# A transformer block with modulated LayerNorms: the attention gate row in a tile and a transfer of its own

## The chip, the cores and the metric

The kernel runs on one core of a Trainium2 chip. The metric is the device time of one execution in microseconds, as the median of several runs. All times in this document are microseconds unless marked ns.

## What is computed

For each of 32 batch entries with 256 tokens of 128 values (cut from the reference):

```python
mod = (_silu(c) @ wmod).reshape(32, 6, 1, -1)
sa, ca, ga, sb, cb, gb = (mod[:, n] for n in range(6))
ga = (2 * (ga >= 0) - 1) * jnp.maximum(jnp.abs(ga), 0.25)
gb = (2 * (gb >= 0) - 1) * jnp.maximum(jnp.abs(gb), 0.25)
h = _layernorm(x) * (1 + ca) + sa
x = x + ga * attn(h)       # rmsnorm, 16 causal heads of 64, sigmoid head gates, @ Wout
h = _layernorm(x) * (1 + cb) + sb
x = x + gb * ffn(h)        # SwiGLU MLP with bias bd, plus experts chosen by product keys
```

The six modulation rows of a batch entry are one value for each of the 128 features and hold for all its tokens. `ga` scales the output of the attention before the residual is added. The output bias `bd` of the MLP is inside the second gate, so the kernel forms `gb * bd` once (the row called GD) and adds it to the new residual.

## The kernel before

**Rows of the modulation.** All modulation rows are computed once at the start and stored to a DRAM tensor, `mods_dram`, of 32 by 7 rows of 128 values: SA, CA, GA, GD, GB and a pair of columns, in this order. In each batch the sync engine (SP) loads from it, broadcast over the 128 partitions: `modA` (SA and CA, for the first LayerNorm), `modB` (GA and GD: 1 KB per partition, 128 KB in all), `modC` (GB, 64 KB) and `col` (the second LayerNorm's columns). There is one buffer of each, so each load waits until the batch before has been read out of it.

**The pipeline.** The batches run in a software pipeline: each engine has a function `body(i)`, called for i from -1 to 32, with the work of one more body woven into the last call; the middle (from 3 on) is a hardware loop. Body i does the projections, scores and the softmax of batch i, the output projection and the second LayerNorm of batch f = i - 1, the experts and the MLP of batch g = i - 2, and the first LayerNorm of batch i + 1. Within a body the order of the work of each engine is written out by hand; semaphores tie the engines together. Matmul results go to four shared PSUM banks, `pW0` to `pW3`, in a fixed order of jobs (`order`); a job may begin when the job before it in its bank has been released. For this change it matters that the value projection `V 4` takes the bank of `GU 3` (the last of four gate and up projections), which VectorE releases with `gate_product(3)`.

**Around the gate.** On VectorE (the function under `@block.vector`) the order of body i is ... `row_max(3)`, `gated_down(0)` (line 1151), `invert(2)` (line 1124), `gate_attention()` (line 1182), `gate_product(3)` (line 1165), `add_residual()` (line 1191), `invert(3)`, `stats2()` (line 1197), `coefficients(2)`, `coefficients(3)`, `aggregate2()` (line 1205), `normalise(2)`, `normalise(3)` (line 1142), `choose(1, 1)` (line 1268, half of the expert masks of the second token block), `ln1(center1)` (line 1004), `gated_down(1)`, `ln1(scale1)` (line 1017), `row_max(4)` (line 1117). `gate_attention` waits for `modB` and for the output projection (`project_out`, line 1685 on TensorE) and multiplies the PSUM bank by row 0 of `modB`. `add_residual` adds `x_res`, the token rows loaded again for this purpose, writes `x2` and releases the bank.

After `aggregate2` GpSimd computes the reciprocal standard deviation (`rstd2`, lines 566, 567, 569 and 571), ScalarE scales the rows with it (`rows2`, line 784), and TensorE transposes them (line 1585). GpSimd's order in a body is `products(0)` (line 515), `candidates()`, `products(1)`, `weigh(0)` (line 524), `add_heads(0)` (lines 531 and 534), `add_bias()` (line 588), `fold(0)` (lines 540 and 544), `rstd1()`, `rstd2()`, `weigh(1)`, `add_heads(1)`, `rms1()` (line 558), `fold(1)`, `shift_top()`. `add_bias` adds row 1 of `modB` (GD) to `x2` of batch g and writes `x2g`, which the last step of batch g adds to the MLP's output.

**The sync queue.** SP's body i issues in this order, each step behind the waits that stand before it: (line 433) `x_in` of batch i + 2 behind `xr_ready`, (line 425) `modA` of i + 2, (line 442) `x_res` of batch i behind the release of the output projection's bank for batch i - 1, that is behind `add_residual`, (line 445) `col` of batch i behind `h2T_high`, (line 453) the store of the output of i - 2 behind the release of bank job `y`, (line 455) `modC` of i - 1, and last (line 460) `modB` of batch i behind `x2g_ready` of batch i - 1. The gate row of batch i is first read by VectorE's body i + 1 and the GD row by GpSimd's body i + 2. `add_bias` of batch i - 1, for which line 460 waits, belongs to GpSimd's body i + 1: the sync queue's body i so ends in the middle of the other engines' body i + 1, shortly ahead of the gate of batch i.

Of the kernel before, what the change touches and what calls it, by code (L numbers as in the profile page):

```python
# [12 lines left out]
ALU = mybir.AluOpType  # L13
# [3 lines left out]
B, N, D = 32, 256, 128  # L17
P = 128
TB = N // P
# [25 lines left out]
SA, CA, GA, GD, GB, COL = range(NMOD - 1)  # L45


def program(nc, x, norm_w, Wq, Wkv, Wout, Wgate, fWg, fbg, fWu, fbu, fWd, fbd, fWq, keys,
            down, up, cond, wmod, out):
    ctx = ExitStack()  # L50
    with ctx:
        def sb(name, shape, dt=F32):
            return ctx.enter_context(nc.sbuf_tensor(name, shape, dt))

        def sem(name):
            return ctx.enter_context(nc.semaphore(name))
# [42 lines left out]
        mods_dram = nc.dram_tensor("mods_dram", [B, NMOD * D], F32, kind="Internal").ap()  # L99
# [2 lines left out]
        x_in = sb("x_in", [P, TB, D])  # L102
        x_res = sb("x_res", [P, TB, D])
        modA = sb("modA", [P, 2, D])
        modB = sb("modB", [P, 2, D])
        col = sb("col", [P, 2])
        modC = sb("modC", [P, 1, D])
        st1 = sb("st1", [P, TB, 6])
# [18 lines left out]
        x2 = sb("x2", [P, TB, D])  # L127
        x2g = sb("x2g", [P, TB, D])
# [64 lines left out]
        def ev(name, n):  # L193
            s = sem(name)
            per[name] = (s, n)
            return name

        def at(name, batch, k):

            return batch * per[name][1] + k  # L200

        def S(name):
            return per[name][0]

        x_loaded, res_loaded = ev("x_loaded", 16), ev("res_loaded", 16)
        col_loaded = ev("col_loaded", 16)
        modA_loaded, modB_loaded, modC_loaded = ev("modA_loaded", 16), ev("modB_loaded", 16), ev("modC_loaded", 16)
        out_stored = ev("out_stored", 16)
        ln1_chain, inverse_ready = ev("ln1_chain", LN1_LINKS), ev("inverse_ready", NP)
        head_chain, tail_chain = ev("head_chain", HEAD_LINKS), ev("tail_chain", TAIL_LINKS)  # L210
# [178 lines left out]
        def run(eng, body, first=3, tail=1):  # L389


            for i in range(-1, first):
                body(i)
            with eng.Fori(first, B - tail) as i:
                body(i)
            for i in range(B - tail, B + 1):
                body(i)
# [3 lines left out]
        @block.sync  # L401
        def _(sp):

            sp.dma_start(x_in[:, :, :], x[0:1].rearrange("o (k p) d -> p (o k) d", p=P)).then_inc(S(x_loaded), 16)
            sp.dma_start(nw[:, :], norm_w.rearrange("(d o) -> d o", o=1), allow_slow_non_contiguous=True).then_inc(load_nw, 16)
            sp.dma_start(w_qkv[:, 0:2 * P], Wq[:, 0:2 * P]).then_inc(load_pairs, 16)
            sp.dma_start(w_qkv[:, DI:DI + 2 * P], Wkv[:, 0:2 * P]).then_inc(load_pairs, 16)
            for a in range(2):
                sp.dma_start(fwq_sb[:, :, a, :], fWq[:, a * RH * KD:(a + 1) * RH * KD].rearrange("d (h n) -> d h n", h=RH)).then_inc(load_keys, 16)
            sp.dma_start(key_sb[:, :, :], keys.rearrange("h k p n -> k h (p n)")).then_inc(load_keys, 16)  # L410
            sp.dma_start(w_qkv[:, 2 * P:DI], Wq[:, 2 * P:DI]).then_inc(load_q, 16)
            sp.dma_start(w_qkv[:, DI + 2 * P:2 * DI], Wkv[:, 2 * P:DI]).then_inc(load_k, 16)
            sp.dma_start(w_qkv[:, GV:GV + H], Wgate).then_inc(load_gv, 16)
            sp.dma_start(w_qkv[:, GV + H:], Wkv[:, DI:2 * DI]).then_inc(load_gv, 16)
            sp.dma_start(down_sb[:, :, :], down.rearrange("(c p) d -> p c d", p=P)).then_inc(load_down, 16)
            sp.dma_start(w_out[:, :, :], Wout.rearrange("(j p) n -> p j n", p=P)).then_inc(load_w, 16)
            sp.dma_start(w_g[:, :], fWg).then_inc(load_w, 16)
            sp.dma_start(w_u[:, :], fWu).then_inc(load_w, 16)
            sp.dma_start(b_g[:, :], fbg.rearrange("(c p) -> p c", p=P), allow_slow_non_contiguous=True).then_inc(load_w, 16)
            sp.dma_start(b_u[:, :], fbu.rearrange("(c p) -> p c", p=P), allow_slow_non_contiguous=True).then_inc(load_w, 16)  # L420
            sp.dma_start(w_d[:, :, :], fWd.rearrange("(c p) n -> p c n", p=P)).then_inc(load_w, 16)
            sp.dma_start(w_up[:, :, :], up.rearrange("(c p) n -> p c n", p=P)).then_inc(load_w, 16)

            def load_modA(b):
                sp.dma_start(modA[:, :, :].rearrange("p m d -> p (m d)"),
                             mods_dram[bass.ds(b, 1), SA * D:(CA + 1) * D].broadcast_to([P, 2 * D])).then_inc(S(modA_loaded), 16)

            def body(i):
                w = Work(sp, i)
                if w.live(2):  # L430

                    sp.wait_ge(S(xr_ready), at(xr_ready, i + 1, 1))
                    sp.dma_start(x_in[:, :, :], x[bass.ds(i + 2, 1)].rearrange("o (k p) d -> p (o k) d", p=P)).then_inc(S(x_loaded), 16)
                    if isinstance(i, int) and i == -1:
                        sp.wait_ge(su_dve, SU_LINKS)
                        sp.dma_start(mods_dram, mods[:, :, :].rearrange("b m d -> b (m d)")).then_inc(mods_stored, 16)
                        sp.wait_ge(mods_stored, 16)
                    load_modA(i + 2)
                if w.live(0):
                    if w.live(-1):  # L440
                        w.wait_released("op")
                    sp.dma_start(x_res[:, :, :], x[bass.ds(i, 1)].rearrange("o (k p) d -> p (o k) d", p=P)).then_inc(S(res_loaded), 16)
                    if w.live(-1):
                        sp.wait_ge(S(h2T_high), at(h2T_high, i - 1, 1))
                    sp.dma_start(col[:, :], mods_dram[bass.ds(i, 1), COL * D:(COL + 2) * D].rearrange("o (d m) -> d (o m)", m=2)).then_inc(S(col_loaded), 16)
                if w.live(-2):
                    if isinstance(i, int) and i > B:
                        for k in range(TB):
                            w.wait_released("y", k)
                            sp.dma_start(out[Z, k * P:(k + 1) * P, :], yo[:, k, :]).then_inc(S(out_stored), 16)  # L450
                        return
                    w.wait_released("y")
                    sp.dma_start(out[bass.ds(i - 2, 1)].rearrange("o (k p) d -> p (o k) d", p=P), yo[:, :, :]).then_inc(S(out_stored), 16)
                if w.live(-1):
                    sp.dma_start(modC[:, :, :].rearrange("p m d -> p (m d)"),
                                 mods_dram[bass.ds(i - 1, 1), GB * D:(GB + 1) * D].broadcast_to([P, D])).then_inc(S(modC_loaded), 16)
                if w.live(0):
                    if w.live(-1):
                        sp.wait_ge(S(x2g_ready), at(x2g_ready, i - 1, 1))
                    sp.dma_start(modB[:, :, :].rearrange("p m d -> p (m d)"),  # L460
                                 mods_dram[bass.ds(i, 1), GA * D:(GD + 1) * D].broadcast_to([P, 2 * D])).then_inc(S(modB_loaded), 16)

            run(sp, body, tail=2)
            body(B + 1)
            sp.wait_ge(S(out_stored), at(out_stored, B, 16))

        @block.gpsimd
        def _(pool):
# [24 lines left out]
            def body(i):  # L493
                w = Work(pool, i)
                f, g = i - 1, i - 2
# [86 lines left out]
                def add_bias():  # L582
                    if w.live(-2):
                        w.wait_released("op", 0, g)
                        pool.wait_ge(S(modB_loaded), at(modB_loaded, g, 16))
                        if w.live(-3):
                            w.wait_released("y", 0, g - 1)
                        nc.gpsimd.tensor_tensor(x2g[:, :, :], x2[:, :, :], modB[:, 1:2, :].broadcast_to([P, TB, D]),
                                                ALU.add).then_inc(S(x2g_ready), 1)

                if isinstance(i, int) and i == 0:
# [27 lines left out]
                weigh(0)  # L619
                add_heads(0)  # L620
                add_bias()
                fold(0)
                rstd1()
# [350 lines left out]
        def _(dve):  # L974
# [130 lines left out]
            def body(i):  # L1105
                w = Work(dve, i)
                f, g = i - 1, i - 2
# [68 lines left out]

                def gate_attention():
                    if w.has("op"):
                        dve.wait_ge(S(modB_loaded), at(modB_loaded, f, 16))
                        w.wait_full("op")  # L1180
                        o = w.bank("op")[:, 0:N].rearrange("p (k d) -> p k d", k=TB)
                        nc.vector.tensor_tensor(o, o, modB[:, 0:1, :].broadcast_to([P, TB, D]), ALU.mult).then_inc(S(head_chain), 1)

                def add_residual():
                    if w.has("op"):
# [806 lines left out]
```

## Time and profile before

| | us |
|---|---|
| median of 3 runs (lowest, highest) | 1395.2 (1394.33, 1395.93) |
| the profiled execution's own time | 1397.2 |
| its span, first to last instruction | 1395.3 |

| engine | busy, us | share |
|---|---|---|
| TensorE matmuls (PE) | 1354.7 | 97% |
| TensorE weight loads (PEld) | 1161.5 | 83% |
| VectorE (DVE) | 1251.7 | 90% |
| ScalarE (ACT) | 1261.1 | 90% |
| GpSimd (POOL) | 1067.2 | 76% |

The granted TensorE clock is 0.995 of full speed over the span, and the DMA engines moved 20 GB/s in the mean. The profile is one execution. Busy times are sums of instruction durations; matmul ends are modelled, so a busy PE is not PE at its peak. Waits are inferred from semaphore events: idle time of an engine just ahead of an instruction, put down to what ended it.

### The profile page before, as it was taken

What the parts mean: (1) busy time and instruction counts of PE and PEld (TensorE: products, weight loads), DVE (VectorE), ACT (ScalarE), POOL (GpSimd) and SP (SyncE); (2) the same over time, 40 slices, a digit from 0 to 9 for tenths busy, and PEclk for the clock granted to TensorE, in tenths of its full rate; (3) what the DMA queues carried; (4) which work ended last, traced back from release to release, by engine and by line L of the source; (5) the groups of instructions that cost most, each with busy time, mean ns of one, the idle gap of its engine ahead of it and who ended that gap; (6) DMA issues with size and microseconds to landing.
All of it is one profiled execution on the core that took longest, in us unless ns stands there. A gap on an engine that the chain in (4) does not pass through costs nothing. (4 is left out here: it accounts for less than half of the span.)

```text
span 1395.3 us, 39507 instructions
## 1 busy us (share of the span) xinstructions
PE 1354.7 (97%) x11491; PEld 1161.5 (83%) x11491; DVE 1251.7 (90%) x5314; ACT 1261.1 (90%) x4084; POOL 1067.2 (76%) x1252
## 2 busy tenths in 40 slices
PE   7799999999999999999999999999999999999998
PEld 4578888888888888888888888888888888888878
DVE  5579999999999999999999999999999999999977
ACT  5789999999999999999999999999999999999985
POOL 2148887888787888787888888888888887878770
PEclk9999999999999999999999999999999999999999
DMA  4000000000000000000000000000000000000000
GB/s 137 16 15 21 9 18 21 17 21 19 9 17 21 18 19 20 11 14 21 20 17 21 13 11 21 21 17 21 15 9 21 21 17 21 15 9 24 10 15 11
DMA packets 51041, 27.74 MB, mean 20 GB/s; under 512 B 10336, under 2 KB 50208, under 8 KB 51008
## 3 DMA queue, kind: packets, MB, share of 16 engines
q1 hardware_dynamic: 50768, 26.91, 7.3%
q10 hardware_dynamic: 240, 0.43, 0.1%
q8 instruction: 16, 0.26, 0.1%
q14 instruction: 17, 0.14, 0.0%
HBM read 23.02 MB, written 4.31 MB: 20 GB/s over the span
## 5 line engine op out<-in xcount | busy, mean ns | idle before, releaser
L692 ACT ACTIVATE pS<-pS,nmx 128x128 f32<-128x128 f32 (+1 forms) x1024 | 405.5, 500 | 17.8 <-DVE nmx L1117 16.5
L524 POOL TENSOR_TENSOR fexp<-fexp,fsum 128x512 f32<-128x512 f32 x240 | 306.3, 1307 | 75.0 <-DVE fexp L1268 75.0
L1117 DVE CUSTOM_DVE_ANT_0 pS<-pS,mask 128x128 f32<-128x128 f32 (+1 forms) x1024 | 333.6, 393 | 27.9 <-PE pS L1629 23.7
L692 ACT ACTIVATION_READ_ACCUMULATOR pS<-pS,nmx 128x1 f32 x1024 | 253.3, 256 | 0.0
L515 POOL TENSOR_TENSOR fsum<-ex 128x512 f32<-128x512 f32 x248 | 251.8, 1047 | 0.0
L1142 DVE TENSOR_TENSOR p_sb<-pS,coef 128x256 f32<-128x256 f32 (+2 forms) x512 | 206.7, 451 | 5.7
L1639 PE MATMUL pS<-ident,p_sb 128*128 128x128 f32 x1536 | 204.1, 276 | 4.3 <-DVE p_sb L1142 2.2
L684 ACT COPY pT<-pS 128x768 f32<-128x768 f32 x256 | 201.4, 850 | 6.4 <-PE pS L1639 6.2
L1639 PEld LDWEIGHTS pS<-ident,p_sb 128*128 128x128 f32 x1536 | 171.0, 141 | 27.3 <-DVE p_sb L1142 12.4
L672 ACT COPY qk<-pW 128x512 f32<-128x512 f32 x256 | 155.1, 606 | 8.4 <-PE pW L1573 3.8
L531 POOL TENSOR_TENSOR fexp<-fexp 128x512 f32<-128x512 f32 x120 | 158.7, 1343 | 4.7
L1654 PE MATMUL pW<-pT,v 128*64 128x256 f32 x1024 | 161.2, 393 | 0.4 <-ACT pT L684 0.4
L1571 PE MATMUL pW<-xT_high,s_qkv_high 128*128 128x256 f32 x512 | 155.7, 304 | 0.4 <-DVE xT_low L1171 0.2
L1629 PE MATMUL pS<-qk 64*128 64x256 f32 x1024 | 155.8, 379 | 0.0
L1268 DVE TENSOR_SCALAR fexp<-fsum,top,rz 128x512 f32<-128x512 f32 x240 | 148.5, 672 | 1.1
L1117 DVE DVE_READ_ACCUMULATOR2_ANT nmx<- 128x1 f32 x1024 | 147.6, 144 | 0.0
L1572 PE MATMUL pW<-xT_low,s_qkv_high 128*128 128x256 f32 x512 | 144.4, 282 | 0.0
L1573 PE MATMUL pW<-xT_high,s_qkv_low 128*128 128x256 f32 x512 | 144.2, 282 | 0.0
L1685 PEld LDWEIGHTS pW<-w_out,aoT 128*128 128x128 f32 x1024 | 116.7, 192 | 11.0 <-issue 10.7
L1685 PE MATMUL pW<-w_out,aoT 128*128 128x128 f32 x1024 | 122.8, 278 | 0.4 <-DVE g_t L1165 0.4
L1625 PE MATMUL pS<-qk 64*128 64x128 f32 x1024 | 114.4, 299 | 7.9 <-ACT pT L684 7.1
L1625 PEld LDWEIGHTS pS<-qk 64*128 64x128 f32 x1024 | 86.7, 186 | 42.0 <-issue 20.8
(211 smaller groups left out, 3716.4 us busy)
## 6 DMA issues: line engine op xcount, KB each, us to landing
x_in<-in_L_attn_tokens SPq DMA_DIRECT2D x32, 128.0 KB, 2.1
x_res<-in_L_attn_tokens SPq DMA_DIRECT2D x32, 128.0 KB, 3.0
modB<-mods_dram SPq DMA_DIRECT2D x32, 128.0 KB, 2.9
modA<-mods_dram SPq DMA_DIRECT2D x31, 128.0 KB, 3.1
out<-yo SPq DMA_DIRECT2D x31, 128.0 KB, 1.9
modC<-mods_dram SPq DMA_DIRECT2D x32, 64.0 KB, 3.0
fsum<-in_L_attn_Wkv SPq DMA_DIRECT2D x1, 512.0 KB, 6.5
w_out<-in_L_attn_Wout SPq DMA_DIRECT2D x1, 512.0 KB, 7.3
```

Source lines behind the costliest of these rows:

```text
L515: ins = nc.gpsimd.tensor_tensor(fsum[:, k, h], ex[:, k, h, 0:NX].unsqueeze(2).broadcast_to([P, NX, NK]), ex[:, k, RH + h, :].unsqueeze(1). ...
L524: ins = nc.gpsimd.tensor_tensor(fexp[:, k, h, :], fexp[:, k, h, :], fsum[:, k, h].rearrange("p i j -> p (i j)"), ALU.mult)
L531: ins = nc.gpsimd.tensor_tensor(fexp[:, k, h, :], fexp[:, k, h, :], fexp[:, k, h + 1, :], ALU.add)
L684: nc.scalar.copy(pT[:, p % 2], pS[:, p % 2, :, 0:SW]).then_inc(S(pT_ready), 1)
L692: ins = nc.scalar.activation(ps, ps, ACT.Exp, bias=nmx[:, p % 2, h, k:k + 1], scale=-1.0, accum_out=den(p)[:, h, k:k + 1])
L1117: ins = nc.vector.tensor_tensor_reduce(out=ps, in0=ps, in1=mask[:, (1 - k) * P:2 * P], scale=-1.0, scalar=LARGEST, op0=ALU.add, op1=ALU.mi ...
L1142: ins = nc.vector.tensor_tensor(o, pS[:, p % 2, mine, cols_of(k)], coef[:, p % 2, mine, k:k + 1].broadcast_to(o.shape), ALU.mult)
L1625: mm(ps[:, h, 0:P], qk[r, p % 4, 0:P], qk[r, p % 4, N:N + P], start=True, stop=True, skip_group_check=True)
L1629: ins = mm(ps[:, h, P:SW], qk[r, p % 4, P:N], qk[r, p % 4, N:2 * N], start=False, stop=True, skip_group_check=True)
L1639: ins = tp(pS[:, p % 2, h, b * P:(b + 1) * P], p_sb[:, p % 2, h, b * P:(b + 1) * P], ident[:, :])
L1654: mm(bank[h * DH:(h + 1) * DH, lo:hi], v[:, 0, hd], pT[:, p % 2, h, 0:2 * P], start=True, stop=False, skip_group_check=True)
L1685: ins = mm(w.bank("op")[:, k * D:(k + 1) * D], aoT[:, p, k * P:(k + 1) * P], w_out[:, p, :], start=p == 0, stop=p == NP - 1)
```

## The change

The gate row GA gets a tile of its own, `modG`, with a semaphore of its own, and a transfer that the sync queue issues right behind that of `x_res`. `modB` keeps only the row GD and its place in the queue. VectorE's `gate_attention` waits for and reads `modG`; GpSimd's `add_bias` reads row 0 of the shorter `modB`.

```diff
-        modB = sb("modB", [P, 2, D])
+        modG = sb("modG", [P, 1, D])
+        modB = sb("modB", [P, 1, D])
...
+        modG_loaded = ev("modG_loaded", 16)
...
                     if w.live(-1):
                         w.wait_released("op")
                     sp.dma_start(x_res[:, :, :], x[bass.ds(i, 1)].rearrange("o (k p) d -> p (o k) d", p=P)).then_inc(S(res_loaded), 16)
+                    sp.dma_start(modG[:, :, :].rearrange("p m d -> p (m d)"),
+                                 mods_dram[bass.ds(i, 1), GA * D:(GA + 1) * D].broadcast_to([P, D])).then_inc(S(modG_loaded), 16)
                     if w.live(-1):
                         sp.wait_ge(S(h2T_high), at(h2T_high, i - 1, 1))
...
                     if w.live(-1):
                         sp.wait_ge(S(x2g_ready), at(x2g_ready, i - 1, 1))
                     sp.dma_start(modB[:, :, :].rearrange("p m d -> p (m d)"),
-                                 mods_dram[bass.ds(i, 1), GA * D:(GD + 1) * D].broadcast_to([P, 2 * D])).then_inc(S(modB_loaded), 16)
+                                 mods_dram[bass.ds(i, 1), GD * D:(GD + 1) * D].broadcast_to([P, D])).then_inc(S(modB_loaded), 16)
...
-                        nc.gpsimd.tensor_tensor(x2g[:, :, :], x2[:, :, :], modB[:, 1:2, :].broadcast_to([P, TB, D]),
+                        nc.gpsimd.tensor_tensor(x2g[:, :, :], x2[:, :, :], modB[:, 0:1, :].broadcast_to([P, TB, D]),
                                                 ALU.add).then_inc(S(x2g_ready), 1)
...
                 def gate_attention():
                     if w.has("op"):
-                        dve.wait_ge(S(modB_loaded), at(modB_loaded, f, 16))
+                        dve.wait_ge(S(modG_loaded), at(modG_loaded, f, 16))
                         w.wait_full("op")
                         o = w.bank("op")[:, 0:N].rearrange("p (k d) -> p k d", k=TB)
-                        nc.vector.tensor_tensor(o, o, modB[:, 0:1, :].broadcast_to([P, TB, D]), ALU.mult).then_inc(S(head_chain), 1)
+                        nc.vector.tensor_tensor(o, o, modG[:, 0:1, :].broadcast_to([P, TB, D]), ALU.mult).then_inc(S(head_chain), 1)
```

## Rows read from the trace of the kernel before

**Rows 1.** The page: busy time, share of the span and instructions of each engine.

```profile
PE 1354.7 (97%) x11491; PEld 1161.5 (83%) x11491; DVE 1251.7 (90%) x5314; ACT 1261.1 (90%) x4084; POOL 1067.2 (76%) x1252
```

**Rows 2.** Waits: engine, tile, line, waited for: us in total, times, longest.

```profile
DVE pW L1182 <- DMA modB<-mods_dram: 22.3, 28, 1.1
...
PEld pW L1571 <- DVE g_t L1165: 12.9, 28, 0.8
...
PE pW L1571 <- DVE g_t L1165: 7.2, 28, 0.5
...
POOL ve L566 <- DVE mv L1205: 21.6, 31, 7.8
...
DVE pS L1124 <- ACT pS L692: 46.0, 34, 1.6
```

**Rows 3.** Timeline, several engines, 693 to 713: start, us, instruction [idle before, releaser].

```profile
693.59 3.84 PE L1685 MATMUL pW<-w_out,aoT 128*128 128x128 f32 x32
...
694.43 0.74 POOL L588 TENSOR_TENSOR x2g<-x,modB 128x256 f32<-128x256 f32 x1
...
695.34 0.33 SPq L460 DMA_DIRECT2D modB<-mods_dram  x1
...
697.30 0.19 DVE L1124 RECIPROCAL pS<-pS 128x4 f32<-128x4 f32 x1
698.23 0.43 DVE L1182 TENSOR_TENSOR pW<-pW,modB 128x256 f32<-128x256 f32 x1 [0.73 <-DMA modB<-mods_dram]
...
699.03 0.19 PEld L1571 LDWEIGHTS pW<-s_qkv_high,xT_high 128*128 128x128 f32 x1 [0.40 <-DVE g_t L1165]
...
700.35 0.23 POOL L566 TENSOR_SCALAR ve<-mv 128x2 f32<-128x2 f32 x1 [0.38 <-DVE mv L1205]
...
700.96 0.71 POOL L569 TENSOR_TENSOR rs<-ve,expo 128x2 f32<-128x2 f32 x1
...
705.38 0.30 DVE L1117 CUSTOM_DVE_ANT_0 pS<-pS,mask 128x128 f32<-128x128 f32 x1
...
712.86 0.19 POOL L558 TENSOR_SCALAR me<-ms 128x2 f32<-128x2 f32 x1 [1.08 <-DVE ms L1032]
```

**Rows 4.** Timeline of VectorE: the first and last of the 28 gates that wait.

```profile
155.69 0.43 DVE L1182 TENSOR_TENSOR pW<-pW,modB 128x256 f32<-128x256 f32 x1 [0.71 <-DMA modB<-mods_dram]
...
1282.08 0.43 DVE L1182 TENSOR_TENSOR pW<-pW,modB 128x256 f32<-128x256 f32 x1 [0.74 <-DMA modB<-mods_dram]
```

**Rows 5.** Timeline of the sync queue, 674 to 681: start, us, issue.

```profile
674.84 0.38 SPq L442 DMA_DIRECT2D x_res<-in_L_attn_tokens  x1
675.42 0.33 SPq L445 DMA_DIRECT2D col<-mods_dram  x1
680.17 0.41 SPq L453 DMA_DIRECT2D out<-yo  x1
```

**Rows 6.** The page's DMA issues: tile, count, KB each, median us to landing.

```profile
modB<-mods_dram SPq DMA_DIRECT2D x32, 128.0 KB, 2.9
...
modC<-mods_dram SPq DMA_DIRECT2D x32, 64.0 KB, 3.0
```

**Rows 7.** Timeline, several engines, 109 to 129: the batch without the wait.

```profile
109.81 3.84 PE L1685 MATMUL pW<-w_out,aoT 128*128 128x128 f32 x32
...
113.76 0.43 DVE L1182 TENSOR_TENSOR pW<-pW,modB 128x256 f32<-128x256 f32 x1
...
116.76 0.89 POOL L569 TENSOR_TENSOR rs<-ve,expo 128x2 f32<-128x2 f32 x1
117.07 1.00 DVE L1268 TENSOR_SCALAR fexp<-fsum,top,rz 128x512 f32<-128x512 f32 x2
...
121.24 0.30 DVE L1117 CUSTOM_DVE_ANT_0 pS<-pS,mask 128x128 f32<-128x128 f32 x1 [0.26 <-PE pS L1629]
...
128.73 0.19 POOL L558 TENSOR_SCALAR me<-ms 128x2 f32<-128x2 f32 x1 [1.41 <-DVE ms L1032]
```

## The prediction

> **What bounds the kernel now.** I read first the page's busy shares: TensorE is busy 97% of the span, so nothing big stands idle [rows 1]. Then the waits. VectorE stands idle 22.3 us in 28 batches for the transfer of modB ahead of the attention gate (line 1182); TensorE's weight queue waits as often, 12.9 us (7.2 us in the matmul rows), for the SwiGLU product that VectorE runs right behind that gate (line 1165, which frees a PSUM bank for the next value projection); GpSimd waits for the second LayerNorm's statistics, which also follow the gate (21.6 us over 31 times, of which one is 7.8 us of the start-up: 0.46 us per batch) [rows 2].
>
> Then one batch in order of time [rows 3]. GpSimd's add_bias (line 588) starts at 694.43 and ends at 695.17; only then may the sync queue overwrite modB, which it issues at 695.34; VectorE has finished what stands ahead of the gate at 697.49 (697.30 and 0.19) and starts the gate at 698.23, when the transfer has landed. Call 697.49 "ready". Bank 1 is freed late, so that the value projection begins at 699.03; GpSimd begins the reciprocal root at 700.35 and the next chain at 712.86; VectorE begins the maxima of the fifth score block at 705.38. The waits close a loop: the gate, the statistics, GpSimd, the row scaling on ScalarE, scores and exponentials, VectorE (46.0 us of waits for ScalarE in the reciprocals, [rows 2]), the expert masks, GpSimd's weighting and add_bias, the transfer, and the gate again. Every link is waited for by the next, so the transfer lies on the loop that sets the period. From the first waiting gate (155.69) to the last (1282.08) there are 27 periods of 41.72 us, and 28 gates that wait 0.80 us each in the mean [rows 4].
>
> **The change part by part.**
> Attention gate row: it is now loaded into modG right behind the residual rows x_res. In the batch that is gated at 698.23 those rows were issued at 674.84 [rows 5]. The new transfer would be issued 0.6 us later, at about 675.4, and land 3 us behind that, since the modC transfer of just this size and kind takes 3.0 us [rows 6]: about 678.4, and 19 us ahead of ready. It needs no wait of its own: the queue has already waited for the release of the out-projection bank, which comes with the residual add, behind the last read of modG. So the wait of 22.3 us for a transfer goes entirely. If x_res came late, modG would too, but its wait shows nowhere now.
>
> Bias row: modB keeps its place and its wait for add_bias, with half the bytes. Its next reader is add_bias one period on: the transfer issued at 695.34 lands by 698.3 and is wanted some 38 us later. Nothing.
>
> The additional transfer: one more issue of 0.33 us on the sync queue with its register moves, 0.6 us in all by the spacing of its neighbours [rows 5]. Queued behind it are the col transfer (issued 675.42, read by ScalarE only in the next batch) and the store of the output, for which the queue waits until 680.17 anyway [rows 5]. The cover is that wait, over 4 us. The bytes are unchanged. Nothing.
>
> Two transfers for one is where a rule speaks against the change. The rows first: 64 KB take 3.0 us and 128 KB take 2.9 us [rows 6], so that a halved transfer saves no time and the second one is a whole 3 us more. The Trainium skill, "DMA: Bandwidth & Descriptors", section "Anatomy of one DMA", says the same: some 2.0 us of every DMA are fixed, whatever its size. Were that part paid on the path, 32 batches would make it 64 us, an estimate from that page; by the rows it is paid 19 us before anybody asks.
>
> What is late next. With the wait gone VectorE runs the gate at ready, 0.80 us earlier, but the ways beside it were less late. TensorE can only gain its own idle time, 12.9 us over 28, that is 0.46 us, of which some hundredths are an ordinary step; GpSimd 0.46 us [rows 2], since before the reciprocal root it has work of its own. The price of this is to be had from a row: there is one full batch in which the gate does not wait, at 113.76 [rows 7]. Measured from ready, the fifth block's maxima start there at 7.48 us (121.24 less 113.76) against 7.89 us (705.38 less 697.49), now with an idle 0.26 us for TensorE's scores, and GpSimd's next chain at 14.97 against 15.37 [rows 3, 7]. So a wait of 0.73 us costs the loop 0.40, and 0.33 to 0.34 of every wait is covered by other work. The rest of a longer wait counts in full, as nothing else covers it.
>
> The sum: 22.3 us less 28 times 0.34 us (9.5 us) gives 12.8 us. From this I take 0.6 us off. The out-projection ends at 697.43 (693.59 and 3.84), only 0.06 us before ready [rows 3], and 0.11 us before in the free batch [rows 7]; a semaphore hop may now show there, between nothing and 0.04 us per batch (1.1 us). 12.2 us stay. The start-up and the last two batches have no such wait and keep their lengths.
> The bounds: from below 7.2 us, all that the matmul rows show as idle behind the late bank; from above 22.3 us, the whole wait. A second reading lies between: the free batch took 41.22 us from its ready (113.76) to the next one (155.69 less 0.71), against 41.72; 28 times 0.50 us is 13.9 us. I take 12.2 because that batch is still in the fill of the pipeline and its later half may be short for another reason.
>
> The span of the profiled execution is 1395.3 us and its own time 1397.2 us; they would become 1383.1 and 1385.0. The median of the runs is 1395.2 us, 2.0 below the profiled execution, and becomes 1383.0. A measurement of this kernel can tell some 0.2%, or 2.8 us, from no change.
>
> **The rivals.**
> Given back in part: VectorE and GpSimd meet differently. In the free batch the mask product (line 1268) starts at 117.07 while GpSimd's power (line 569) has been running since 116.76, and that takes 0.89 us instead of 0.71 [rows 3, 7]. My sum has this once, but other pairs may meet. At 0.2 us per batch the gain is 12.2 less 5.6, 6.6 us: 1388.6 us. 13%.
>
> The whole wait is worth its length: only if TensorE's and GpSimd's own idle times were shadows of the same loop and shrank with it. The gain is 22.3 us, 1372.9 us. Against it stands the free batch with its 0.40 for 0.73. 3%.
>
> No change: the gate waits for something as late as the transfer, the out-projection first of all, or the loop is closed by another way of equal length. For it speaks the 0.06 us by which the projection ends before ready; against it that it does so before ready, not after, in both batches. 1395.2 us. 6%.
>
> Slower: the earlier VectorE work holds up GpSimd's four small instructions behind the statistics, which release the row scaling and with it TensorE. Two of them (lines 569 and 571) would each be held for one half of the mask product, which takes 1.00 us for two [rows 7]: 1.0 us in place of the 0.18 seen. The 0.82 us more, less the 0.44 us gained (12.2 over 28), lose 0.38 us per batch: 28 times that is 10.6 us, 1405.8 us. It decides from a delay of 0.44 us beyond the one seen. Against it: the mask product beside line 569 took its usual 1.00 us, and GpSimd only 0.18 more. 4%.
> The Trainium skill has a rule for this, "SBUF — State Buffer", section "SBUF: two separate sides": VectorE and GpSimd share one pair of ports, and who starts first holds it for a whole instruction. Taken to the letter the product would have waited for line 569 to end; the row shows both overlapping, so the trace bears the rule out only as a stretch.
>
> **How the numbers follow.** Forecast 74%, with 1380 to 1386 us of its own: 15 us if the free batch's 0.50 us and a little more hold, 9 us if the covered part is nearer 0.46. The three others that gain or keep and the one that loses have 13, 3, 6 and 4%. The range 1379.5 to 1389.5 us takes in the forecast and most of the part given back. Faster by over 0.2%: 74, 13 and 3, that is 90%; within it 6%; slower 4%.
>
> **What would show it.** Right: no wait for modG or modB at line 1182, the wait at the value projection for line 1165 gone, waiting gates' spacing 41.72 down to 41.25 to 41.35, the fifth block's maxima 7.5 us behind the gate with a short wait for TensorE, modG issued some 20 us before its gate. Wrong: a new wait at line 1182 for TensorE of 0.3 us or more, lines 566 to 571 taking over 0.5 us more together, or a spacing under 41.1 or over 41.6.

## The result and the profile after

| | before, us | after, us |
|---|---|---|
| median of 3 runs (lowest, highest) | 1395.2 (1394.33, 1395.93) | 1386.53 (1384.91, 1387.01) |
| the profiled execution | 1397.2 | 1386.53 |
| its span | 1395.3 | 1384.7 |
| granted TensorE clock | 0.995 | 0.995 |

The ratio is 0.9934, with a 95% interval of 0.9921 to 0.9947: 8.7 us faster by the medians, 10.7 by the two profiled executions (10.6 by their spans). 12.2 us had been forecast. The second pair is the one that the sum was made for, so the traces are compared with it. Three executions among all that follow (two of the kernel before, one of the kernel with rstd1 earlier) were slow runs of 4.6 to 7.5 ms, and no ratio holds them.

The busy times of the page of the kernel after, the line that answers to [rows 1]:

```profile
PE 1352.0 (98%) x11491; PEld 1159.9 (84%) x11491; DVE 1252.9 (90%) x5314; ACT 1260.0 (91%) x4084; POOL 1071.3 (77%) x1252
```

The same instructions are there, and GpSimd's take 4.1 us longer together; the reason comes below. From here on, a line number of the kernel after is four more than that of the same code before.

The same page's DMA issues, the lines that answer to [rows 6]:

```profile
modG<-mods_dram SPq DMA_DIRECT2D x32, 64.0 KB, 2.9
...
modB<-mods_dram SPq DMA_DIRECT2D x32, 64.0 KB, 2.8
...
modC<-mods_dram SPq DMA_DIRECT2D x32, 64.0 KB, 3.0
```

The waits of the kernel after (engine, tile, line, waited for: us in total, times, longest), to be held against [rows 2]:

```profile
DVE pS L1128 <- ACT pS L696: 45.2, 33, 1.6
DVE pS L1121 <- PE pS L1633: 33.6, 44, 4.5
...
ACT h L788 <- POOL mr L575: 14.4, 30, 1.6
...
POOL ve L570 <- DVE mv L1209: 10.3, 3, 9.0
```

The gate (now line 1186) has no wait for a transfer any more, and the value projection (now line 1575) none for the SwiGLU product. GpSimd's wait for the second LayerNorm's statistics fell from 31 times to 3. In their place VectorE waits longer for TensorE's scores ahead of the maxima (line 1121; 23.7 us over 15 times in the kernel before), and ScalarE for GpSimd's row statistics (line 788): 14.4 us over 30 times, 0.48 us each, against 8.3 us over 30 times before.

One batch in order of time, timeline of several engines, 669 to 708 (start, us, instruction [idle before, releaser]); it answers to [rows 3] and [rows 5]:

```profile
669.48 0.38 SPq L444 DMA_DIRECT2D x_res<-in_L_attn_tokens  x1
670.06 0.33 SPq L445 DMA_DIRECT2D modG<-mods_dram  x1
670.58 0.33 SPq L449 DMA_DIRECT2D col<-mods_dram  x1
674.80 0.41 SPq L457 DMA_DIRECT2D out<-yo  x1
...
688.22 3.84 PE L1689 MATMUL pW<-w_out,aoT 128*128 128x128 f32 x32
...
691.93 0.18 DVE L1128 RECIPROCAL pS<-pS 128x4 f32<-128x4 f32 x1
692.17 0.43 DVE L1186 TENSOR_TENSOR pW<-pW,modG 128x256 f32<-128x256 f32 x1
...
693.88 0.25 DVE L1209 BATCH_NORM_AGGREGATE mv<-st 128x2 f32<-128x6 f32 x2
693.88 0.72 POOL L556 TENSOR_TENSOR rs<-ve,expo 128x2 f32<-128x2 f32 x1
694.58 0.23 POOL L570 TENSOR_SCALAR ve<-mv 128x2 f32<-128x2 f32 x1
695.19 0.86 POOL L573 TENSOR_TENSOR rs<-ve,expo 128x2 f32<-128x2 f32 x1
695.48 0.99 DVE L1272 TENSOR_SCALAR fexp<-fsum,top,rz 128x512 f32<-128x512 f32 x2
696.13 0.39 POOL L575 TENSOR_TENSOR mr<-nm,rs 128x2 f32<-128x2 f32 x1
696.55 0.88 ACT L788 ACTIVATE h<-x,mr,rs 128x128 f32<-128x128 f32 x2 [0.43 <-POOL mr L575]
...
699.72 0.30 DVE L1121 CUSTOM_DVE_ANT_0 pS<-pS,mask 128x128 f32<-128x128 f32 x1 [0.34 <-PE pS L1633]
```

The gate row is issued 0.58 us behind the residual rows and 22.1 us ahead of its gate, and the store of the output is still issued 4.2 us behind the last of those loads, so the queue's slack was not used up. The fifth block's maxima start 7.55 us behind the gate (699.72 less 692.17). The loop has a new member. GpSimd is busy with the first LayerNorm's power (line 556) until 694.6, though the second's statistics have been there since 694.13. Then its power for the second (line 573) takes 0.86 us instead of 0.71 while VectorE's mask product runs beside it from 695.48 (28 times 0.15 is 4.2 us, which accounts for the 4.1 by which GpSimd's busy time grew), and the row scaling waits 0.43 us for GpSimd. Ready is at 692.11 here (691.93 and 0.18), 0.06 us ahead of the gate. Counted from ready, GpSimd's chain starts 0.39 us earlier than before (2.47 against 2.86, 700.35 less 697.49), and the maxima 0.28 (7.61 against 7.89).

Two regular gates, 26 periods apart, of VectorE's timeline in the kernel after:

```profile
154.63 0.43 DVE L1186 TENSOR_TENSOR pW<-pW,modG 128x256 f32<-128x256 f32 x1
...
1229.69 0.43 DVE L1186 TENSOR_TENSOR pW<-pW,modG 128x256 f32<-128x256 f32 x1
```

That is 41.35 us per period against 41.72 [rows 4]: 0.37 us less, and 28 times 0.37 is 10.4 of the span's 10.6 us. What is left nearly cancels: the gate of the free batch comes 0.36 us earlier (113.40 against 113.76), and the last full period is 0.39 us longer than before (41.87 against 41.48).

### The profile page after: what moved, and what is told of

Same layout as the page of the kernel before. It is cut to its first block and busy times, and to the rows that moved or that the text cites. A ratio compares the mean times of both kernels' runs of the same rounds, so it can differ in the third digit from the quotient of the medians.

```text
span 1384.7 us, 39593 instructions
## 1 busy us (share of the span) xinstructions
PE 1352.0 (98%) x11491; PEld 1159.9 (84%) x11491; DVE 1252.9 (90%) x5314; ACT 1260.0 (91%) x4084; POOL 1071.3 (77%) x1252
## 5 line engine op out<-in xcount | busy, mean ns | idle before, releaser
L1121 DVE DVE_READ_ACCUMULATOR2_ANT nmx<- 128x1 f32 x1024 | 143.2, 140 | 0.0
```

The source lines that it names most:

```text
L1121: ins = nc.vector.tensor_tensor_reduce(out=ps, in0=ps, in1=mask[:, (1 - k) * P:2 * P], scale=-1.0, scalar=LARGEST, op0=ALU.add, op1=ALU.mi ...
```

## The experiments

All times are medians in us; the ratio is to runs of the kernel before on the same chip, whose medians lay between 1395.4 and 1396.8. "Period" is the mean spacing of regular gates over 26 or 27 batches, in one trace each. The two traces of the changed kernel differ by 0.05 us in it (41.35 and 41.40), so a smaller difference between two rows says nothing by itself.

| | median | ratio (95%) | period |
|---|---|---|---|
| before, repeated | 1395.56 | 0.9995 (0.9986 to 1.0004) | 41.70 |
| after, repeated | 1386.07 | 0.9923 (0.9909 to 0.9936) | 41.40 |
| gate row split, issued late | 1394.42 | 0.9984 (0.9975 to 0.9994) | 41.65 |
| after, rstd1 earlier | 1380.06 | 0.9887 (0.9872 to 0.9902) | 41.19 |
| the same, repeated | 1382.35 | 0.9901 (0.9886 to 0.9917) | 41.19 |
| before, rstd1 earlier | 1395.64 | 0.9993 (0.9983 to 1.0003) | 41.72 |
| after, one product ahead of the gate | 1384.95 | 0.9922 (0.9899 to 0.9946) | 41.32 |
| after, two products ahead of the gate | 1394.84 | 0.9992 (0.998 to 1.0004) | 41.65 |
| after, one more transfer | 1387.99 | 0.9941 (0.992 to 0.9962) | 41.42 |
| before, product ahead of gate | 1390.3 | 0.9962 (0.995 to 0.9975) | 41.46 |
| after, product ahead of gate | 1386.54 | 0.993 (0.9912 to 0.9949) | 41.34 |
| after, both reorderings | 1382.91 | 0.9906 (0.9892 to 0.992) | 41.23 |

### Both kernels again

No edit. Expected of the kernel before:

> The kernel before, once more. Theory: four of the 28 waits at the gate were 1.0 us or longer in the profiled execution shown, the others 0.71 to 0.86, which is why that execution took 2.0 us more than the median; another execution has its own number of long waits, and its time is some 1394 us plus what the waits have over 0.73 us. Rival: the 2.0 us came from elsewhere, and the sum of the waits does not go with the time.

And of the kernel after:

> The changed kernel, once more, to narrow the gain. Theory: 28 periods shorter by 0.30 to 0.37 us, a ratio of 0.992 to 0.994 (1384 to 1387 us). Rival: the 12.2 us of the forecast are there and the three runs were unlucky: 0.991 or less.

The ratio of after to before came out at 0.9923, the first at 0.9934; both intervals hold both. Of the kernel before, 21 runs have a median of 1396.2, one us over the three runs that the prediction started from. The profiled execution of the kernel before took 1397.0 us here, 1.5 above its median. Its trace waits 22.1 us at the gate in 28 batches, as much as the first, so the expectation that longer waits set a profiled execution apart was wrong. What goes with the time in these 11 executions is the granted clock: the four at 0.995 took 1396.6 to 1397.0 us, the six at 0.996 took 1395.2 to 1395.6, and the one at 0.999 took 1394.2. For the changed kernel the executions at 0.996 took 1384.9 to 1385.4 us, and those at 0.995 took 1386.1 to 1387.0 (one at 0.998 took 1386.8 and doesn't fit). At 0.996 on both sides the change so gains some 10 us. The relation is looser in the other 21 executions of the kernel before: medians of 1396.5 us at 0.995 and 1395.8 at 0.996, with single ones that overlap. Medians of few executions that differ by 1 or 2 us are to be read with this in mind.

### Is it the place or the tile? The gate row split, but issued late

```diff
                     sp.dma_start(x_res[:, :, :], x[bass.ds(i, 1)].rearrange("o (k p) d -> p (o k) d", p=P)).then_inc(S(res_loaded), 16)
-                    sp.dma_start(modG[:, :, :].rearrange("p m d -> p (m d)"),
-                                 mods_dram[bass.ds(i, 1), GA * D:(GA + 1) * D].broadcast_to([P, D])).then_inc(S(modG_loaded), 16)
...
                     if w.live(-1):
                         sp.wait_ge(S(x2g_ready), at(x2g_ready, i - 1, 1))
+                    sp.dma_start(modG[:, :, :].rearrange("p m d -> p (m d)"),
+                                 mods_dram[bass.ds(i, 1), GA * D:(GA + 1) * D].broadcast_to([P, D])).then_inc(S(modG_loaded), 16)
```

> Two tiles and two transfers as in the change, but the gate row's transfer is issued where modB's is, behind add_bias. Theory (only the place counts): the gate waits again, 0.7 us or a little more in 28 batches, and the time is that of the kernel before, 1395 us, ratio 1.000. Rival (a shorter transfer or the split itself helps): the waits shrink with the halved bytes and the ratio is 0.997 or less.

1394.42 us. The waits and the timeline of this kernel:

```profile
DVE pW L1186 <- DMA modG<-mods_dram: 20.2, 28, 1.0
```

```profile
693.39 0.33 SPq L462 DMA_DIRECT2D modG<-mods_dram  x1
693.94 0.33 SPq L464 DMA_DIRECT2D modB<-mods_dram  x1
...
696.22 0.43 DVE L1186 TENSOR_TENSOR pW<-pW,modG 128x256 f32<-128x256 f32 x1 [0.66 <-DMA modG<-mods_dram]
```

The wait is back, 0.72 us in the mean instead of 0.80, and nearly the whole time with it. Of the 9 to 10 us that the change brings, the earlier place brings all but about 2. Those 2 us are there, though, between theory and rival (0.9984, the interval under 1; 0.05 to 0.07 us of the period): the page has the half transfer land in 2.8 us instead of 2.9, and from its issue to the gate it is 2.83 us here (696.22 less 693.39) against 2.89 (698.23 less 695.34, [rows 3]), and on the loop that counts.

### What covers part of the wait? One or two products ahead of the gate

The gate product is also written into a tile that nobody reads, once or twice, each time 0.34 us more ahead of the gate proper (the line with scr2 is in the second kernel alone).

```diff
+                        nc.vector.tensor_tensor(scr[:, :, :], o, modG[:, 0:1, :].broadcast_to([P, TB, D]), ALU.mult)
+                        nc.vector.tensor_tensor(scr2[:, :, :], o, modG[:, 0:1, :].broadcast_to([P, TB, D]), ALU.mult)
                         nc.vector.tensor_tensor(o, o, modG[:, 0:1, :].broadcast_to([P, TB, D]), ALU.mult).then_inc(S(head_chain), 1)
```

> The changed kernel, with the gate's product written once more into an unused tile ahead of the gate itself, some 0.34 us more on VectorE at this place in each batch. The output is the reference's. Theory (0.38 us of a wait at the gate is covered by TensorE and GpSimd): nothing to 2 us more than the changed kernel, 1386 to 1388 us. Rival (every delay counts at its length): 31 times 0.34 us, 10.5 us more, 1397 us.

> The same with two such extra products, some 0.68 us more on VectorE ahead of the gate. Theory (0.38 us covered, the rest counts in full): 31 times 0.30 us, 9 us more than the changed kernel, 1395 to 1396 us. Rival (every delay counts at its length): 21 us more, 1407 us.

The first costs next to nothing: 1384.95, against 1386.5 and 1386.1 without it. (Two of its four executions ran at a clock of 0.998; the two at 0.996 and 0.995 took 1385.8 and 1387.8 us, more than the changed kernel at those clocks, so a gain isn't shown.) The second costs 0.33 us of the period and 9.9 us of the median more than the first. That is the step in the price of a delay that the prediction had taken from the one free batch: the first 0.34 us covered, what lies beyond in full. The timeline of the kernel with one product, VectorE and GpSimd:

```profile
689.57 0.43 DVE L1187 TENSOR_TENSOR scr<-pW,modG 128x256 f32<-128x256 f32 x1
689.91 0.42 DVE L1188 TENSOR_TENSOR pW<-pW,modG 128x256 f32<-128x256 f32 x1
...
692.02 0.23 POOL L571 TENSOR_SCALAR ve<-mv 128x2 f32<-128x2 f32 x1
...
692.64 0.71 POOL L574 TENSOR_TENSOR rs<-ve,expo 128x2 f32<-128x2 f32 x1
...
693.21 0.99 DVE L1274 TENSOR_SCALAR fexp<-fsum,top,rz 128x512 f32<-128x512 f32 x2
693.43 0.37 POOL L576 TENSOR_TENSOR mr<-nm,rs 128x2 f32<-128x2 f32 x1
...
697.05 0.30 DVE L1122 CUSTOM_DVE_ANT_0 pS<-pS,mask 128x128 f32<-128x128 f32 x1
```

GpSimd's chain for the second LayerNorm starts right behind its first (no wait), as it did without the delay, so the delay isn't seen there. And VectorE's mask product now starts at 693.21, when the power has only 0.14 us to run: it takes 0.71 us, not 0.86. GpSimd's next instruction, the last ahead of the row scaling, ends 0.59 us behind the product's start (693.80 less 693.21) and not 1.04 (696.52 less 695.48). So the row scaling starts 4.27 us behind the first of the two products (693.84 less 689.57), earlier than the 4.38 us behind the gate (696.55 less 692.17) without the delay. The maxima come 7.48 us behind the first of the two products, not 7.55. ScalarE's wait for GpSimd at the row scaling is down from 14.4 us to 9.1. With two products the waits of before are back, the projection's for the SwiGLU product and GpSimd's for the statistics, as [rows 2] had them:

```profile
POOL ve L571 <- DVE mv L1212: 22.8, 32, 9.7
...
PEld pW L1578 <- DVE g_t L1170: 11.2, 30, 0.5
...
PE pW L1578 <- DVE g_t L1170: 5.0, 30, 0.3
```

### Is GpSimd's chain the next bound? rstd1 ahead of fold(0)

```diff
                 add_bias()
-                fold(0)
                 rstd1()
+                fold(0)
                 rstd2()
```

Applied to the kernel after, run twice:

> The changed kernel, with GpSimd's rstd1 moved ahead of fold(0), into the 1.65 us for which GpSimd waits there anyway. Theory (what is late next is GpSimd's own work ahead of the reciprocal root, lines 548, 554 and 556, which now ends later than the statistics): the root starts up to 0.3 us earlier behind the gate, TensorE's transposes start 0.1 to 0.2 us earlier, then TensorE itself binds; the period goes from 41.35 to some 41.2 us and the time to some 1382 us, ratio to before 0.990. Rival (TensorE or the out-projection's end binds already): the time stays at that of the changed kernel, 1386 us.

> The changed kernel with rstd1 ahead of fold(0), once more, as the swapped form came out 2.9 us slower on another chip run than this one. Theory (the swap is worth nothing either way and what differed is the executions): ratio 0.989 to 0.991, 1380 to 1383 us. Rival (the swap costs 2 to 3 us): 0.9887 again, 1380 us or less.

And to the kernel before:

> The kernel before, with GpSimd's rstd1 moved ahead of fold(0) and nothing else. Theory (in the kernel before, GpSimd waits 0.4 us for the statistics anyway): nothing, ratio 1.000 within 0.1%. Rival (GpSimd's order is worth something by itself): 0.997 or less.

In the kernel after it gains 6.0 and 3.7 us more (1380.06 and 1382.35 against 1386.07, the repeated one's median; most executions behind the first ran at 0.997 or 0.998 of the clock, most behind the second at 0.996, and those at 0.996 took 1381.9 to 1382.6 in both); in the kernel before it gains nothing (0.9993). This is the best version that was run, 0.9887 and 0.9901. The timeline of the first of them:

```profile
687.45 0.31 POOL L544 TENSOR_SCALAR wsum<-wsum,tot 128x1 f32<-128x1 f32 x1 [0.52 <-ACT junk L771]
...
688.17 0.43 DVE L1186 TENSOR_TENSOR pW<-pW,modG 128x256 f32<-128x256 f32 x1
...
690.29 0.23 POOL L570 TENSOR_SCALAR ve<-mv 128x2 f32<-128x2 f32 x1 [0.83 <-DVE mv L1209]
...
690.89 0.72 POOL L573 TENSOR_TENSOR rs<-ve,expo 128x2 f32<-128x2 f32 x1
...
695.56 0.30 DVE L1121 CUSTOM_DVE_ANT_0 pS<-pS,mask 128x128 f32<-128x128 f32 x1 [0.17 <-PE pS L1633]
```

GpSimd's chain starts 2.12 us behind the gate instead of 2.41, now as soon as the statistics are there; its power takes 0.72 us; the maxima follow at 7.39 us instead of 7.55. Those 0.16 us are the period's difference (41.35 less 41.19), and 28 of them are 4.5 us. The row scaling starts 0.46 us earlier behind the gate (3.93 us, median of the batches, against 4.39), of which TensorE takes back 0.30. So in the kernel after GpSimd's own work ahead of the chain lies on the loop, and in the kernel before, where GpSimd idles for the statistics, it does not.

### Gaining without the transfer: the SwiGLU product ahead of the gate

```diff
                 invert(2)
-                gate_attention()
                 gate_product(3)
+                gate_attention()
                 add_residual()
```

> The kernel before with one line moved on VectorE: gate_product(3) runs ahead of gate_attention instead of behind it, that is inside the wait for modB. Theory (what the wait costs is the 0.34 us by which the statistics behind the gate are later than TensorE and GpSimd need): the idle time at the gate falls by 0.34 to some 0.4 us per batch, the gate itself starts no earlier, but the residual add and the statistics do, and the period falls from 41.72 to some 41.4 us, ratio 0.993 to 0.995 with the transfers as they were. Rival (the period is set by the landing of the transfer itself, whatever VectorE does in the meantime): 1.000.

> The changed kernel with the same line moved. Theory (nothing waits at the gate but some 0.03 us for the out-projection's end, which the product now covers): the period goes from 41.35 or 41.40 down by 0.00 to 0.04 us, up to 1 us in all, ratio to before 0.991 to 0.993. Rival (the attention gate coming 0.34 us later is itself late): 0.995 or more.

> Both: the changed kernel with rstd1 ahead of fold(0) and with gate_product(3) ahead of the gate. Theory (with rstd1 moved, TensorE's own order sets the transposes, 5.28 us behind the gate, and the gate waits 0.03 us for the out-projection): equal to the kernel with rstd1 moved or up to 1 us less, 1379 to 1380.5 us, ratio 0.988 to 0.989. Rival (the statistics are then late again): 0.991 or more.

In the kernel before, 1390.3 us: 5 to 6 us gained with the transfer left alone, less than the 7 to 10 expected (0.9962, against 0.993 to 0.995). Its waits and timeline:

```profile
POOL ve L566 <- DVE mv L1205: 15.6, 30, 7.8
...
DVE pW L1182 <- DMA modB<-mods_dram: 12.9, 28, 0.7
```

```profile
692.69 0.19 DVE L1124 RECIPROCAL pS<-pS 128x4 f32<-128x4 f32 x1
692.78 0.41 DVE L1165 SCALAR_TENSOR_TENSOR g_t<-g_t,pW 128x256 f32<-128x256 f32 x1
...
693.75 0.43 DVE L1182 TENSOR_TENSOR pW<-pW,modB 128x256 f32<-128x256 f32 x1 [0.55 <-DMA modB<-mods_dram]
694.22 0.42 DVE L1191 TENSOR_TENSOR x<-pW,x_res 128x256 f32<-128x256 f32 x1
```

The product fills the time in which VectorE would wait, and the wait falls from 22.3 to 12.9 us. The product ends 0.31 us behind the reciprocal's end (693.19 less 692.88), where the value projection before had the bank only 1.54 us behind it (699.03 less 697.49, [rows 3]). The statistics come only 0.20 us earlier behind the gate (1.76 us against 1.96, medians), and not the product's 0.34: the residual add has to wait for the gate itself, and starts 0.47 us behind it (694.22 less 693.75). In the kernel after, where there is no wait to fill, the same exchange changes nothing that can be told from noise: 1386.54, and with rstd1 earlier 1382.91 against 1380.06 and 1382.35. The last was expected at 1379 to 1380.5 us and missed that by over 2 us; that is why the kernel with rstd1 earlier was run a second time, whose 0.9901 leaves the exchange a cost of 1 us or none (0.04 us of the period). The gate starts 0.18 us later behind ready, and with less between it and the statistics the maxima come as early as without (7.58 against 7.60 us behind ready, medians).

### Is a transfer free? One more of the same

A third tile, modX, takes a second copy of the gate row in one more transfer right behind modG's, and the gate waits for both; nobody reads modX.

```diff
+                    sp.dma_start(modX[:, :, :].rearrange("p m d -> p (m d)"),
+                                 mods_dram[bass.ds(i, 1), GA * D:(GA + 1) * D].broadcast_to([P, D])).then_inc(S(modX_loaded), 16)
...
                         dve.wait_ge(S(modG_loaded), at(modG_loaded, f, 16))
+                        dve.wait_ge(S(modX_loaded), at(modX_loaded, f, 16))
```

> The changed kernel, with a third transfer of the gate row into an unused tile right behind the second; the gate waits for both. Theory (a further early transfer is free): 1386 us, ratio to the changed kernel 1.000. Rival (each additional transfer costs something, on the sync queue or in the DMA engines): 32 times 0.1 us or more, 1389 us or more.

1387.99 us, 0.9941 with an interval of 0.992 to 0.9962 that takes in the changed kernel's 0.9934 and 0.9923. The DMA issues of this page:

```profile
modG<-mods_dram SPq DMA_DIRECT2D x32, 64.0 KB, 3.6
modX<-mods_dram SPq DMA_DIRECT2D x32, 64.0 KB, 4.0
```

The transfers lengthen each other, and there is no wait for either at the gate; the gate starts 0.26 us behind its reciprocal instead of 0.24. By the medians one more transfer costs 1.5 to 2 us, between the 1386 of the theory and the 1389 of its rival. Its four executions had granted clocks of 0.996 to 0.999, no lower than those of the changed kernel, so the clock doesn't explain it; its period of 41.42 is 0.02 and 0.07 us above theirs. Four executions don't settle whether it costs nothing or some 3 us; a cost of the size of the wait, they exclude.

## Why the prediction was right, and by how much it was off

- **The wait goes entirely.** Right: none at line 1186 for a transfer, modG issued 22.1 us ahead of its gate (20 expected). That the place does it, and not the split, the late split shows.
- **Nothing for the extra transfer.** Right as far as it goes: no wait followed it, and the output's store goes out as long ahead of ready as before (17.31 us against 17.32). The run with one more transfer suggests that it isn't quite free; a cost of some 2 us stays possible.
- **A halved transfer saves no time.** Wrong in the small: 2.8 against 2.9 us, and on the path that is worth some 2 us in all (late split). It had no part in the sum, since the new place takes it off the path. The section "Anatomy of one DMA" of the Trainium skill, "DMA: Bandwidth & Descriptors", which the prediction names beside it, gives its fixed 2.0 us for transfers issued by GpSimd, and these go out on the sync queue; the sum didn't use it.
- **TensorE and GpSimd cover 0.34 us of each wait.** Right in kind, and shown by the two kernels with products ahead of the gate. This is the term that was mis-sized: the free batch gave maxima 7.48 us behind the gate, which it took for ready (it was 0.02 us later); the steady batches of the kernel after have 7.55. The cover so is 0.39 us in place of 0.34 (0.73 less the 0.34 by which 7.55 lies under 7.89), and 28 times 0.05 is 1.4 us. (In the repeated pair the period fell by 0.30 us only, 41.70 to 41.40, so the size is known to some 0.05.) The kernel after has that batch too, in VectorE's timeline from 113 to 121, again at 7.48 us (120.88 less 113.40) with TensorE last; so it differs from a steady batch by being in the fill of the pipeline, as the prediction feared. The row scaling starts as long behind the gate in both (4.39 and 4.38 us); the transposes behind it (line 1589) start at 5.32 us in this batch (118.72) and at 5.39 in the steady ones (697.56), with TensorE idle just before for 0.16 us of which the profile says only "issue". Why TensorE takes 0.07 us longer there stays open.

```profile
113.40 0.43 DVE L1186 TENSOR_TENSOR pW<-pW,modG 128x256 f32<-128x256 f32 x1
...
120.88 0.30 DVE L1121 CUSTOM_DVE_ANT_0 pS<-pS,mask 128x128 f32<-128x128 f32 x1 [0.27 <-PE pS L1633]
```

- **A tie with the out-projection, 0.6 us.** Right in size: from the reciprocal to the gate it is 0.24 us, 0.21 in the free batch; 28 times 0.03 is 0.8 us. That these 0.03 us are the projection's isn't shown: the trace names no wait for it at the gate of a steady batch. The sum, redone per batch: 0.80 less 0.39 less 0.03 is 0.38, beside the 0.37 measured. Counted from ready, the maxima come at 7.95 us before and 7.60 after (means of the batches), and the rest of the period is the same to 0.02 us.
- **The baseline.** The miss of 3.5 us (1386.53 less 1383.0) has two parts. 1.5 us are the sum's: 12.2 against 10.7 by the profiled pair, for which it was made. The other 2.0 us are the medians', whose pair gained 8.7. The larger samples, 1396.2 for the kernel before and 1386.1 for the changed one, give 10.1, so most of these 2 us is the draw of the three runs on either side. The clocks go some way to say how: two of the three executions of the changed kernel, the median among them, ran at 0.995, as the profiled execution of the kernel before did; the clocks of the three behind 1395.2 aren't known. The prediction carried the 2.0 us between profiled execution and median over to the kernel after, where the profiled execution was the median.
- **Given back in part.** The rival's mechanism is there, at less than its price: the power's 0.86 us is the stretch that the sum had already. A second pair meets, GpSimd's last product (line 575) with VectorE's mask product, but it met in the kernel before too (0.38 us there, 0.39 now, 0.20 in a batch without it), so it adds nothing. By time the result (8.7 to 10.7 us) lies between forecast and rival.
- **No change, slower, whole wait.** None of them: the projection still ends ahead of ready, if by 0.05 us; GpSimd's power and the instruction behind it each ended with one half of the mask product, as that rival has it, but most of their length had run beside it: that cost 0.15 and 0.02 us more than before, and not 0.82; and the wait was worth about half its length.

The marks named ahead were met but for a hair: spacing 41.35 and, repeated, 41.40 (41.25 to 41.35 expected), maxima at 7.55 us with a wait of 0.34 us for TensorE. The prediction named TensorE and GpSimd together as what covers; the runs tell them apart. GpSimd's fold(0) and rstd1 stand ahead of the second LayerNorm's chain, and moving one of them away gains 0.16 us per period; after that VectorE still waits 0.17 us for TensorE ahead of the maxima. The profile of before held it in one row: GpSimd had been idle for only 0.38 us at line 566 [rows 3], where the gate was to come 0.73 us earlier.

## What to carry to other kernels

Taking away a wait on the critical loop gains its length only until the next-latest way decides: before pricing it, read how long the other engines stand idle in the same stretch, and look for one batch in which the wait is missing, best a steady one. Where that cover is an engine's own order of work, as GpSimd's here, removing the wait makes a reordering pay that was worth nothing before. A row that two consumers need at different times is better loaded by two transfers, each issued when its own slot is free.

## What the runs showed of the hardware

- Two small GpSimd instructions end when the VectorE instruction beside them ends. The mask product is two VectorE instructions of 128x512, SBUF to SBUF, of 0.54 us each, which end 0.54 and 0.99 us behind its start. Where it starts 0.27 to 0.36 us into GpSimd's power on 128x2, the power ends 0.57 to 0.58 us behind the product's start, whatever the offset (it takes 0.84 to 0.94 us instead of 0.71). GpSimd's next instruction, 0.20 us without the mask product, then takes 0.39 and ends at 1.04. Where the product starts 0.57 us into the power, the power keeps its 0.71 us, and the next one ends at 0.59. The product keeps its 0.99 us throughout, and GpSimd's 0.23 us on the statistics are the same beside VectorE's products that read PSUM. The first batch has no mask product there; GpSimd's timeline of the kernel after:

```profile
76.42 0.20 POOL L575 TENSOR_TENSOR mr<-nm,rs 128x2 f32<-128x2 f32 x1
```

- So what the prediction read as a stretch of 0.18 us is a wait for the end of a VectorE instruction, and it goes in steps. It is part of how a delay of 0.34 us on VectorE could cost next to nothing: it moved the product's start from 0.29 to 0.57 us into the power. The Trainium skill, "SBUF — State Buffer", section "SBUF: two separate sides", calls the ports that the two engines share an exclusive lock: a GpSimd instruction, or a VectorE instruction in a two-port mode (or with two inputs in SBUF, against a GpSimd instruction that reads SBUF), has them for its whole length if it started first. The ends above agree with VectorE's side of that. GpSimd's side doesn't show: the product started 0.29 us into the power (695.48 less 695.19) and kept its length. No run shows in which mode the product ran.
- A broadcast load of 64 KB landed 2.8 to 3.1 us behind its issue, one of 128 KB in 2.9 to 3.2. With modX's load put between those of modG and col, the 64 KB of modG took 3.6 us instead of 2.9, those of modX 4.0, and the 1 KB of col 3.6 instead of 2.6.
- Executions of one kernel spread with the granted clock: 1396.6 to 1397.0 us at 0.995, 1395.2 to 1395.6 at 0.996, 1394.2 at 0.999 (the kernel before, one series of 11 executions).
